# Value matrices made once per batch and spread by a 0/1 matrix; constants first, statistics of x in halves

## What is computed

```python
def _L0_xattn_ref(q, k, v, mask, Wq, bq, Wk, bk, Wv, bv, Wo, bo):
    ...
    qh = split_heads(q, Wq, bq)      # q = layernorm(x)
    kh = split_heads(k, Wk, bk)      # k = v = the context, 77 rows of 256
    vh = split_heads(v, Wv, bv)
    scores = jnp.einsum('hbsd,hbtd->hbst', qh, kh) * scale
    scores = jnp.where(mask == 0, jnp.float32(-1000000000.0), scores)
    attn = jax.nn.softmax(scores, axis=-1)
    out = jnp.einsum('hbst,hbtd->hbsd', attn, vh)
    ...
    return out @ Wo.T + bo
x = x + _L0_xattn_ref(_layernorm(x, axis=-1), ctx_1024, ctx_1024, mask, ...)
x = x + _L0_ffn_ref(_layernorm(x, axis=-1), ...)
```

## Time and profile before

| | |
|---|---|
| median of 3 runs | 969.92 us (968.76 to 970.57) |
| the profiled execution's own time | 965.83 us |
| its span, first to last instruction | 964.2 us |
| mean granted TensorE clock | 0.883 of full |
| busy share of the span: PE, DVE, ACT, POOL | 87%, 53%, 29%, 59% |
| setup, to the first normalisation of the attention | 0 to 79.9 us |
| attention | 79.9 to about 412 us |
| routed experts | about 443 to 870 us |
| shared expert and output | about 870 to 964 us |

### The profile page before, as it was taken

One profiled execution on the slowest core, in us unless ns is written; L12 is line 12 of the kernel. 1 busy time (PEld: TensorE's weight loads), 2 busy tenths in 40 slices (PEclk: granted clock), 3 DMA queues, 4 the chain that ended last, 5 costly groups with the idle time before them and its releaser, 6 DMA issues.

```text
span 964.2 us, 16500 instructions
## 1 busy us (share of the span) xinstructions
PE 843.5 (87%) x4963; PEld 687.4 (71%) x4963; DVE 512.8 (53%) x1629; ACT 279.3 (29%) x595; POOL 567.3 (59%) x470
## 2 busy tenths in 40 slices
PE   4998999999999999404989899999998999878996
PEld 3886888888888888303868777777777877754554
DVE  3502678787778878640444444444444444442656
ACT  0002654545455544102322222222222222210110
POOL 0200056666666766770788888888888888882000
PEclk9555987898888878656999999999999999998999
DMA  9699623333333333385789999999999999978786
GB/s 285 205 368 353 217 96 121 128 114 121 119 128 109 129 118 121 138 222 159 110 152 150 154 148 151 151 154 150 151 153 151 151 153 152 151 102 205 227 261 210
DMA packets 144101, 160.03 MB, mean 166 GB/s; under 512 B 17665, under 2 KB 137093, under 8 KB 144018
## 3 DMA queue, kind: packets, MB, share of 16 engines
q0 software_dynamic: 41952, 59.28, 35.3%
q1 hardware_dynamic: 98824, 96.99, 35.0%
q10 hardware_dynamic: 3242, 2.73, 1.1%
HBM read 70.61 MB, written 84.15 MB: 161 GB/s over the span
## 4 chain that ended last, share of the span: by engine, by line
DMA 28%; POOL 25%; issue 21%; PE 18%; DVE 4%; SPq 2%; ACT 0%; DVEq 0%; POOLq 0%
DMA acc<-work 25%; POOL rows L436 18%; POOL acc L457 7%; PE sc_ps L775 6%; PE sc_ps L585 4%; DVE work L1121 2%; PE sc_ps L586 2%; PE bank L786 2%; DMA rows<-padrow 1%; PE sc_ps L734 1%; SPq L294 1%; DVE wgu L1142 1%; DMA wdn<-in_ctx_t 1%; POOL rstd L442 1%; PE bank L647 0%
## 5 line engine op out<-in xcount | busy, mean ns | idle before, releaser
L457 POOL DMA_INDIRECT acc<-work x224 | 347.8, 1553 | 96.7 <-DVE work L1121 59.5
L1121 DVE TENSOR_SCALAR work<-bank,work 128x256 f32<-128x256 f32 x224 | 108.1, 483 | 225.7 <-DMA acc<-work 222.8
L734 PE MATMUL sc_ps<-wgu,work 128*128 x896 | 215.7, 384 | 11.0 <-ACT work L544 10.4
L436 POOL DMA_INDIRECT rows<-work,dest x192 | 189.2, 985 | 56.9 <-issue 55.6
L734 PEld LDWEIGHTS sc_ps<-wgu,work 128*128 128x128 f32 x896 | 163.0, 192 | 32.1 <-issue 14.2
L544 ACT ACTIVATE work<-sc_ps 128x512 f32<-128x512 f32 x112 | 66.9, 597 | 197.7 <-PE sc_ps L719 197.7
L751 PE MATMUL bank<-wdn,work 128*128 x448 | 116.8, 383 | 2.3 <-DVE work L1105 2.3
L719 PE MATMUL sc_ps<-cst,work 128*128 128x128 f32 x448 | 81.4, 284 | 41.9 <-DMA work<-rows 40.6
L719 PEld LDWEIGHTS sc_ps<-cst,work 128*128 128x128 f32 x448 | 55.2, 142 | 68.2 <-DMA work<-rows 34.3
L442 POOL TENSOR_TENSOR rstd<-var,cst 128x1 f32<-128x1 f32 x32 | 18.1, 564 | 126.9 <-DVE var L929 126.9
L549 ACT ACTIVATE work<-sc_ps 128x256 f32<-128x256 f32 x112 | 43.0, 384 | 143.7 <-PE sc_ps L734 143.7
(11 more groups left out here) (141 smaller groups left out, 1127.8 us busy)
## 6 DMA issues: line engine op xcount, KB each, us to landing
work<-rows SPq DMA_DIRECT2D x224, 144.5 KB, 3.6
wgu<-acc SPq DMA_DIRECT2D x32, 512.0 KB, 6.3
acc<-padrow SPq DMA_DIRECT2D x3, 4224.0 KB, 28.3
wgu<-in_egu SPq DMA_DIRECT2D x4, 2048.0 KB, 16.3
store<-in_x SPq DMA_DIRECT2D x8, 512.0 KB, 8.9
wdn<-in_edn SPq DMA_DIRECT2D x4, 1024.0 KB, 11.3
acc<-work SPq DMA_DIRECT2D x32, 128.0 KB, 1.9
store<-work SPq DMA_DIRECT2D x32, 128.0 KB, 2.0
```

What stands on the lines that cost most here:

```text
L436: pool.indirect_dma_start(rows[:, :], bass.IndirectOffsetOnAxis(ap=dest[:, m % 2, k:k + 1], axis=0), rowb[:, m, :], None).then_inc(scat[m] ...
L457: pool.indirect_dma_start(acc[m % R_ACC][:, :], bass.IndirectOffsetOnAxis(ap=xe[:, m, ROW - 1:ROW].bitcast(u32), axis=0), ye[:, m % R_ACC, ...
L734: last = mm(ps8[2 + m % 2][:, w * 2 * I:(w + 1) * 2 * I], xeT[:, m % 2, (2 * w + k) * P:(2 * w + k + 1) * P], wgu[:, bass.ds(e * 512 + k * ...
L1121: ts(ye[:, r, :], ps8[6 + m % 2][:, w * D:(w + 1) * D], xe[:, 2 * m + w, bass.ds(e + D, 1)], None, ALU.mult).then_inc(S_["ye"], 1)
```

## The change

- `ctx3` and its six loads go. PE makes the value rows of each batch in one product, 77 x 256, with one bias row (three matmuls a batch, twelve in all in place of 120). ACT copies them to `vrows`, PE spreads all four batches to the chunks with ten matmuls by the 0/1 matrix `rep`, and DVE masks them into `vbd` chunk by chunk, ten operations in place of four. The columns of ones are written at the start.
- DVE does the constants, the mask and the nine steps of `bo` (after which it gives `wg_free`) before any statistics of x.
- The statistics, the variance, the power on POOL and `shift1` are made for tiles 0 to 15 and then for 16 to 31. The first normalisation needs only the first half. The second half stands on DVE after the first `shift1` and before the first `row_max`.

```diff
-W_LOADS = 5 + 4 * KT + 3 + 3
+W_LOADS = 5 + KT + 3 + 3
...
-                for i in range(3):
-                    sp.dma_start(ctx3[:, k, :, i * C:(i + 1) * C],
-                                 ctx_t[:, k * P:(k + 1) * P, :].rearrange("b p c -> p b c")).then_inc(S_["ld_w"], 16)
...
-            need(sp, "vbd_ready", 0, B)
+            need(sp, "vbd_ready", 0, B + NCH)
...
+            for half in range(2):
+                mine = slice(half * NT // 2, (half + 1) * NT // 2)
+                need(pool, "var1_ready", half)
+                pool.tensor_tensor(rstd1[:, mine], tmp1[:, 0, mine], const("half_neg")[:, 0:NT // 2],
+                                   ALU.pow).then_inc(S_["rstd1_ready"], 1)
...
-            need(a, "norm1_ready", 0)
+            for b in range(B):
+                need(a, "v_ps", b)
+                a.activation(vrows[0:C, b, :], ps8[b][0:C, 0:D], ACT.Copy).then_inc(S_["vrows"], 1)
...
             for b in range(B):
-                for c in range(NCH):
-                    off, n0 = c * P % C, chunk_head(c) * DH
-                    cols = ps8[b][:, c * 48:c * 48 + 48]
-                    for k in range(KT):
-                        mm(cols, ctx3[:, k, b, off:off + P], wv_sb[:, k, n0:n0 + 48], start=k == 0, stop=False)
-                    last = mm(cols, ones_row, bv_row[0:1, n0:n0 + 48], start=False, stop=True)
-                last.then_inc(S_["v_ps"], 1)
+                for k in range(KT):
+                    mm(ps8[b][0:C, 0:D], ctxT[:, k, b * C:(b + 1) * C], wv_sb[:, k, :], start=k == 0, stop=False)
+                mm(ps8[b][0:C, 0:D], ones_row[:, 0:C], bv_row[0:1, :], start=False, stop=True).then_inc(S_["v_ps"], 1)
             mm(bank[2][:, 0:E], ones_row, gb_row[0:1, :], start=True, stop=True).then_inc(S_["gb_ps"], 1)
+            need(pe, "vrows", 0, B)
+            for c in range(NCH):
+                off, n0 = c * P % C, chunk_head(c) * DH
+                mm(vchunk[c].rearrange("p (b n) -> p b n", b=B), const("rep")[0:C, off:off + P],
+                   vrows[0:C, :, n0:n0 + 3 * DH], start=True, stop=True).then_inc(S_["vchunk_ps"], 1)
...
+            for s in range(2):
+                x_stats(s)
             need(v, "k_ps", 0)
...
+            for s in range(2, SB // 2):
+                x_stats(s)
+            x_variance(0)
             need(v, "gb_ps", 0)
...
+            for c in range(NCH):
+                if c % 2 == 0:
+                    need(v, "vchunk_ps", c + 1)
+                tt(vbd[:, :, c, :, 0:DH], vchunk[c].rearrange("p (b j d) -> p b j d", b=B, j=3),
+                   vm[:, c, :].unsqueeze(1).unsqueeze(3).broadcast_to([P, B, 3, DH]), ALU.mult).then_inc(S_["vbd_ready"], 1)
+            x_shift(0)
+            for s in range(SB // 2, SB):
+                x_stats(s)
+            x_variance(1)
+            x_shift(1)
```

More of the change, by code:

```diff
@@ L182, in build @@
         ctxT, at = carve(wdn, at, [P, KT, B * C])
-        ctx3, at = carve(wdn, at, [P, KT, B, 3 * C])
+        vrows, at = carve(wdn, at, [P, B, D])
         bv_row, at = carve(wdn, at, [P, D])
@@ L226, in build @@
         rk_ps = bank[1][:, 0:E]
+        VB = (0, 1, 2, 3, 7)
         ps8 = [sc_ps[:, i, :] for i in range(4)] + [b[:, :] for b in bank]
-        for name in ("ld_const ld_w ld_gate ld_egu ld_edn ld_mask cst_b k_ps kbd_ready v_ps vbd_ready gb_ps gb_ready "
+        vchunk = [ps8[VB[c // 2]][:, (c % 2) * B * 3 * DH:(c % 2 + 1) * B * 3 * DH] for c in range(NCH)]
+        for name in ("ld_const ld_w ld_gate ld_egu ld_edn ld_mask cst_b k_ps kbd_ready v_ps vrows vchunk_ps vbd_ready gb_ps gb_ready "
                      "top_ends bo_parts mask_ready repb_ready pad_ready pool_go probs_zero setup_read wg_free stats1_ready "
@@ L475, in _ @@
             a.dma_start(gb_row[0:1, :], gate_b.rearrange("(a n) -> a n", a=1)).then_inc(S_["ld_w"], 16)
-            need(a, "norm1_ready", 0)
+            for b in range(B):
+                need(a, "v_ps", b)
+                a.activation(vrows[0:C, b, :], ps8[b][0:C, 0:D], ACT.Copy).then_inc(S_["vrows"], 1)
             def norm1(t, m, s):
+                if t % (NT // 2) == 0:
+                    need(a, "norm1_ready", t // (NT // 2))
                 freed(a, "xT_ps", t, 2)
@@ L592, in _ @@
             pe.wait_ge(S_["kbd_ready"], 2)
-            pe.wait_ge(S_["vbd_ready"], B)
+            pe.wait_ge(S_["vbd_ready"], B + NCH)
             pe.wait_ge(S_["bo_parts"], 9)
@@ L797, in _, with x_stats @@
             tt, ts, red = v.tensor_tensor, v.tensor_scalar, v.tensor_reduce
-            for s in range(SB):
+            me, mo = stats1[:, :, 1], stats1[:, :, 4]
+            ve, vo = stats1[:, :, 2], stats1[:, :, 5]
+            def x_stats(s):
                 v.wait_ge(ld_x[s], 16)
@@ L804, in _ @@
                     last = v.bn_stats(stats1[:, t, :], store[:, t * D:(t + 1) * D])
[L805 to L819, removed]
+                if s % (SB // 2) == SB // 2 - 1:
+                    last.then_inc(S_["stats1_ready"], 1)
@@ new lines, in x_variance @@
+            def x_variance(half):
+                h = slice(half * NT // 2, (half + 1) * NT // 2)
+                need(v, "stats1_ready", half)
+                tt(mean1[:, h], me[:, h], mo[:, h], ALU.add).then_inc(S_["mean1_ready"], 1)
+                tt(tmp1[:, 0, h], me[:, h], mo[:, h], ALU.subtract).then_inc(S_["tmp_ready"], 1)
+                tt(tmp1[:, 1, h], ve[:, h], vo[:, h], ALU.add).then_inc(S_["tmp_ready"], 1)
+                v.wait_ge(S_["tmp_ready"], 4 * half + 2)
+                tt(tmp1[:, 0, h], tmp1[:, 0, h], tmp1[:, 0, h], ALU.mult).then_inc(S_["tmp_ready"], 1)
+                ts(tmp1[:, 1, h], tmp1[:, 1, h], 1.0 / D, EPS, ALU.mult, ALU.add).then_inc(S_["tmp_ready"], 1)
+                v.wait_ge(S_["mean1_ready"], 2 * half + 1)
+                ts(mean1[:, h], mean1[:, h], 0.5, None, ALU.mult).then_inc(S_["mean1_ready"], 1)
+                v.wait_ge(S_["tmp_ready"], 4 * half + 4)
+                v.scalar_tensor_tensor(tmp1[:, 0, h], tmp1[:, 0, h], 0.25, tmp1[:, 1, h], ALU.mult,
+                                       ALU.add).then_inc(S_["var1_ready"], 1)
@@ L822, in _, with x_shift @@
+            def x_shift(half):
+                h = slice(half * NT // 2, (half + 1) * NT // 2)
+                need(v, "rstd1_ready", half)
+                v.wait_ge(S_["mean1_ready"], 2 * half + 2)
+                v.scalar_tensor_tensor(shift1[:, h], mean1[:, h], -1.0, rstd1[:, h], ALU.mult,
+                                       ALU.mult).then_inc(S_["norm1_ready"], 1)
             v.wait_ge(S_["ld_const"], 32)
@@ L826, in _ @@
             v.tensor_copy(regionb[:, :], const("shares")).then_inc(S_["repb_ready"], 1)
+            vm = const("vmask").rearrange("p (c j) -> p c j", c=NCH)
+            for b in range(B):
+                v.tensor_copy(vbd[:, b, :, :, DH], vm).then_inc(S_["vbd_ready"], 1)
             v.wait_ge(S_["ld_mask"], 16)
```

2 lines of the change are left out of this document (removed).

## The result

The changed kernel takes 943.55 us (median of 4 runs, 942.47 to 945.27); the kernel before 969.34 us (4 runs, 965.38 to 970.57). The ratio is 0.9742, 95% interval 0.971 to 0.9774, so 22 to 28 us are gained. The forecast was 947.2 in a range of 938 to 953. The profiled execution has its own time of 945.27 us and a span of 942.5 us.

A forecast was written before the change was run, and what follows sets the result against it. The first scatter bounds the kernel, held by the first x1 store on SP's queue: draining 10.0 + 3.4 us earlier, then about 2 us to land, brings `residual` 22.7 us earlier. 969.92 - 22.7 = 947.2 us, range 938 to 953.

The forecast's parts named there:

- What bounds: Whole kernel: the result depends on how much earlier the first scatter comes; all later stages move as a block.
- Value products: Setup on PE: 120 matmuls of 67.2 us replaced by 12 and 10 matmuls, costing 11.4 to 24.6 us.
- The start of PE: Setup: PE starts between 10 and 13.07 us, and `wg_free` comes by 16.7.
- my hole rival: Setup DMA: weights land only after x, leaving a 5.1 us hole in SP's queue; 952 us, chance 0.12.
- Statistics in halves: DVE before the first `row_max`: 9.8 to 12.7 us instead of 7.4; `row_max` at 37.2 to 56.3.
- The gate: `residual` of tile 2 waits for tile 0's x1 store behind SP's queue: drain at 97.0, `residual` at 99.0.
- The hole: DMA gap around 26 to 35 us closes because `wg_free` no longer waits for x: 10.0 us.
- The six loads: Removed `ctx3` loads, 0.95 MB at 280 GB/s on SP's queue: 3.4 us.
- The sum: Whole kernel: `residual` of tile 2 comes 22.7 us earlier, and the median falls from 969.92 to 947.2 us.
- No gate: First x1 store lands ahead of earlier transfers, so only the setup's start counts: 929 us, chance 0.07.
- slower: Attention after the stop settles in a rhythm with more half-rate time, 1 us a tile: 976 us, chance 0.04.
- The clock: PE's restart after the stop: a 5 us half-rate stretch costs 2.5 us, counted as none; otherwise 949.7 us.

The follow-up runs named there:

- the four of the first group: Four variants of the changed kernel run together on one chip, where the kernel before took 968.5 us; they took 956.51, 949.11, 971.91 and 933.34 us.
- with these loads kept: Changed kernel with the six `ctx3` loads issued again ahead of the mask, read by nothing: 949.11 us, ratio to before 0.9791.
- statistics first: Changed kernel with all 32 statistics and both variances back ahead of the constants, no halves, new value product kept: 956.51 us, ratio to before 0.9868.
- one accumulator's bytes: Changed kernel with one large accumulator's initial rows (4.3 MB) issued in pieces beside the attention tiles, not ahead of the first x1 store: 933.34 us.
- Weights first: Kernel with all accumulators' rows late and second-half statistics in the loop, but SP issues one x load, then waits for the weights: 953.0 against 953.51 us.
- the order alone: Changed kernel with the old 120-matmul value product, keeping constants first and statistics in halves: 971.91 us, ratio to before 1.0035.
- second group: Changed kernel again and three variants with all accumulators' rows late, on another chip: 988.97, 965.14, 967.55 and 961.53 us; the kernel before took 1012.94.

## Why the prediction was right, step by step

- *What bounds.* Right: everything after the first scatter moved as a block. From the first scatter to the end of the span it was 838.0 us before, 839.1 in the changed kernel, and 838.8 to 842.0 in the four of the first group.
- *Value products.* The twelve and ten matmuls took 4.3 + 2.6 + 2.9 + 0.8 = 10.6 us, just under the lower bound of 11.4. The groups of the changed kernel, 0 to 90 us:

```profile
L588 PE MATMUL sc_ps<-wdn 128*77 128x256 f32 x16 | 4.3, 391 | 0.0
L594 PE MATMUL sc_ps<-wdn,cst 77*128 77x192 f32 x16 | 2.9, 333 | 0.3 <-ACT wdn L481 0.3
L589 PE MATMUL sc_ps<-wdn,cst 1*77 1x256 f32 x8 | 2.6, 405 | 0.0
...
L594 PE MATMUL bank<-wdn,cst 77*128 77x192 f32 x4 | 0.8, 326 | 0.0
```

- *The start of PE.* Mis-sized: I had it between 10 and 13.07, it was 14.16, and `wg_free` came at 17.7 where I had 16.7 at the latest. The last thing to land was 0.1 KB of the gate's bias, issued by 6.3 us, for which PE waited till 14.16. This was the mechanism of my hole rival, x in the way of the weights; it was too weak to open a hole, since x itself still filled the queue. My argument against it, that ACT's queue was done by 10 us before, held only while the loads of `ctx3` stood ahead of x. The packets of ACT's queue show it, in 9 to 10 us with these loads kept and in 13 to 14 us in the changed kernel:

```profile
q10 hardware_dynamic: 260, 0.02, 18.1%
```

```profile
q10 hardware_dynamic: 27, 0.00, 2.0%
```

With the loads kept ACT's queue has nothing in 10 to 11, and PE starts at 13.05, when the context has landed. In 6 to 7 us ACT's queue got 0.23 MB beside 0.09 MB of `ctx3`, but 0.13 MB beside 0.17 MB of the mask and x. The Trainium skill, page "DMA: Bandwidth & Descriptors", section "Issuing engines are not separate DMA queues", says that transfers of all issuing engines run on the same 16 and interleave. The trace agrees: both queues moved packets in every us from 3 to 14, and the last 0.1 KB took about 8 us.
- *Statistics in halves.* Right in kind, and near in size: first `row_max` at 38.62 in a range of 37.2 to 56.3, 9.3 us behind the first `norm1` and not 7.4, where I had 9.8 to 12.7. It cost nothing here, hidden by the gate's 26.6 us.
- *The gate.* Right in place and cause: `residual` of tile 2 at 99.71 (forecast 99.0), waiting for the DMA of `acc<-work`. The closeness of the size is in part luck, for two terms erred in opposite ways. Reckoned as in the forecast (332 and 142 of 350 GB/s in 97 to 99), the queue drained at 98.4, 12.0 us earlier than before and not 13.4; and `residual` ran 1.3 us behind that, not 2. The hole gave 9.6 us (statistics first) where the sum had 10.0. The six loads gave 2.4 at the queue's end and 2.0 at `residual` where it had 3.4. I had priced their 0.95 MB at 280 GB/s, the mean of the stretch where they stood; at the 350 GB/s of the full queue they are 2.7 us.
- *The sum.* 22.7 forecast; 21.95 to `residual`, 22.8 to the first scatter, 21.7 in span, 22 to 28 in the measured ratio. The medians are 25.8 us apart, 3.1 more than forecast; the two traces show nothing of that, and it lies in how single executions scatter: I added 4.1 us from the profiled execution to the median, but after the change the profiled execution lies 1.7 us above its median. The 0.85 us between the first two is work that PE had done during the stop: from `residual` to the first scatter it was 4.55 us before and 3.70 now.
- *No gate* and *slower* fell. The cadence of 9.61 us is the old one, and one accumulator's bytes moved the wait by their own time.
- *The clock.* The granted clock was 0.50 in the stop and still 0.50 in 100 to 105, then 0.86 to 110. Windows of the changed kernel:

```profile
90.00:94.00 4.00, 0.00 (x0) 0.00 (x0) 0.00 (x0) 0.00 (x0) 0.00 (x0) 0.50 1.10 350
...
100.00:105.00 5.00, 4.72 (x31) 3.73 (x32) 3.97 (x21) 0.92 (x3) 1.82 (x3) 0.50 0.15 52
105.00:110.00 5.00, 5.00 (x36) 4.50 (x34) 4.59 (x18) 3.17 (x7) 3.79 (x4) 0.86 0.32 123
```

The Trainium skill's page "TensorE: Matmul & The Clock Gate", Part 1, says that the throttled state is the default and that activity releases it. This restart agrees; the setup before does not, where PE was busy for 57.00 of 57.00 us in 22 to 79 at 0.50. The restart did not add the 2.5 us that I worked out as its price, since from the first scatter to the end the changed kernel took only 1.1 us more; the kernel before had its own such stretch there.

The best kernel of the study is the change with the accumulators' first rows beside the tiles and the second half of the statistics in the loop: 0.951 to 0.953 of the kernel before in two groups, where the change alone is at 0.974 to 0.977. Weights first (0.9502) can't be told from it.

## What to carry to other kernels

When a setup becomes much shorter, look for the first thing of the next stage that is queued behind the setup's transfers: here one 128 KB store behind 26 MB of loads and fills took back half of the gain, and moving 13 MB that nobody needed for 400 us, issued in pieces beside the loop, brought most of it back. Two edits can be worth more together than one by one, since each takes away one of two parallel bounds: here the order alone cost 3 us, the cheap product alone gave 12, and both gave 26. Price the second bound as carefully as the first, from bytes and the rate of the full queue.

## What the runs showed of the hardware

- The same kernel differed between the three groups, each on a chip of its own, by more than the change: the kernel before took 968.5, 1012.94 and 1003.0 us, and the ratio of the change stayed (0.974 and 0.977). In the changed kernel of the second group the attention's cadence was (397.0 - 112.2) / 26 = 10.95 us a tile. Beside it is a wait that the first trace of the changed kernel doesn't have: DVE's `place` stood for a product whose record had ended over 2 us before, and the profile names no engine for it. The waits of the changed kernel on that chip, 200 to 360 us:

```profile
DVE place L1033 <- remote: 38.8, 14, 2.8
ACT work L514 <- remote: 26.8, 14, 2.0
```

In the first trace `place` waits 1.0 us at most in this stretch, and for PE. What delays it is open.
- The first matmuls ran slowly although the granted clock was shown as 1.00: in the changed kernel the eight records of 308 columns from 14.16 took 4.03 us, 0.50 each, and the next four, of 256 columns, 0.26 each (1.03 us from 18.02).
- PE's clock fell under the old value product at full busy share (0.50 in 22 to 79 us, busy 57.00 of 57.00), and stayed at 1.00 through the new one (20 to 24 us, busy 4.00 of 4.00).
